# 44 of 80 edge tiles by one-hot products and 36 by gathers, in a two-layer graph kernel on one Trainium2 core

## The chip, the cores and the metric

The kernel runs on one core of a Trainium2 chip. Its engines are TensorE (PE in the profile; PEld are its weight loads), VectorE (DVE), ScalarE (ACT), GpSimd (POOL) and SyncE (SP); SP and POOL issue the DMAs here, and POOL alone the indirect ones (gathers and scatters by a list of row numbers). The metric is the device time of one execution in microseconds, lower is better: the median over the runs shown.

## What is computed

The reference is a two-layer graph transformer for 625 nodes, 512 features and 10,000 edges: layer 0 is a GENConv network, a linear attention and a small mixture of experts, layer 1 a graph attention, a second linear attention and a second mixture of experts, each with layer norms and residual sums. The change touches the scores of the graph attention of layer 1 (8 heads of 64):

```python
hr_src = h_r[:, src]
hr_dst = h_r[:, dst]
diff = hr_dst - hr_src
score = s_src + s_dst + jnp.einsum('hed,hd->he', diff, a_dif) \
    + jnp.einsum('hed,hd->he', jnp.abs(diff), a_abs) \
    + jnp.einsum('hed,hd->he', hr_src * hr_dst, a_prd)
alpha = jax.nn.leaky_relu(score, negative_slope=ALPHA)
m = jax.ops.segment_max(alpha.T, src, num_segments=N)
...
out = jax.ops.segment_sum(msg, src, num_segments=N)
```

The terms in `s_src`, `s_dst`, `a_dif` and `a_prd` are made for all pairs of nodes by dense products. The term with `abs(diff)` is not separable; it is made edge by edge, 125 edges a tile, 80 tiles. A score tile is [125 edges, 8 heads].

## The kernel before, in words

All engines run hand-written instruction streams that wait on semaphores. Five node tiles of 125 rows (`NT`), four column tiles of 128 (`KC`) and eight heads (`H`) make up the dense parts. The stage of the change is the loop over the edges in layer 1, `TURNS = ET // 2 = 40` turns, and each turn makes two tiles, one in each of two ways:

- **By gathers (chain 0).** POOL's `gather(g)` (L654) issues two indirect DMAs (L657) that fetch the rows of `h_r` for the sources (`gs`) and the destinations (`gd`) of 125 edges from the DRAM tensor `table`, four tiles ahead (`GATHERS`). DVE subtracts them (L1822), takes `max(.,0)` times the weights (`weighted_rise`, L1798) and sums each head into a slot of `sc` (`score`, L1806).
- **By one-hot products (chain 1).** DVE makes two one-hot matrices of the edges (L1789, L1792), PE turns their difference (`edge_turn`, L919), ACT copies it to SBUF (L1248), PE multiplies it with `h_r` in two halves, high and low (`edge_product`, L932), and DVE does `weighted_rise` and `score` on the result in PSUM.

POOL then scatters each score tile (`scatter`, L667) to one of two DRAM tables, `pairs_0` from the gathered tiles and `pairs_1` from the products; each table has one row for each pair of nodes. A scatter waits for its score and for the landing of the previous scatter into the same table (`scattered_0`, `scattered_1`), so the scatters of each table form a chain. POOL's order in a turn is: the scatter of chain 0, the two gathers for four turns later, the scatter of chain 1.

Beside the edges PE does the second linear attention: the tables of turns at L91 to L98 say in which turn it makes the keys, queries, values, the context, the heads' outputs, the turned rows for the next stage (`rT`) and the output projection (`PROJECTED`, five tiles `y1`, of which the last two stand behind the last turn). DVE adds each projected tile to `x` (`mix1_out`, L1780 and L1782). These tiles share two PSUM slots in turn, so a tile waits until the one two places before it has been emptied.

When both chains have landed, SP loads the tables back (L532 on), and DVE merges the two with a maximum, head by head (`merge`, L1854), before the softmax over all pairs of nodes (L1869 on).

## Time and profile before

| | |
|---|---|
| median of 3 runs | 1159.93 us (1158.28, 1159.93, 1166.69) |
| the profiled execution | 1156.4 us, of which the span of the trace is 1154.5 |
| PE busy | 1003.5 us (87%), 4204 matmuls |
| DVE busy | 785.5 us (68%) |
| POOL busy | 358.2 us (31%) |
| ACT busy | 325.6 us (28%) |
| edge stage, first gather to last scatter | 698.2 to 920.4 us |
| first merge of the two tables | 934.37 us |
| chain of work that ended last, by engine | PE 47%, DVE 25%, POOL 11%, issue 8%, DMA 7% |

The time of the profiled execution is its span and 1.9 us around it. Times in rows are microseconds from the start of the span. A row of the timeline gives start, length, engine, line, operation, what it writes and reads, and in brackets the idle time of that engine before it with what ended it; rows that follow one another closely are merged ("x8"). The chain of work that ended last is followed back from the last instruction, each step to what released it. "issue" is time in which an engine waited for nothing that the profile shows.

### The profile page before, as it was taken

How to read it: one execution, taken by the hardware profiler on the slowest of the kernel's cores; microseconds unless marked ns; L12 is line 12 of the kernel's file. 1: busy time of each engine (PE TensorE's matmuls, PEld its weight loads, DVE VectorE, ACT ScalarE, POOL GpSimd, SP SyncE). 2: the span in 40 equal slices, each digit the busy share in tenths (PEclk: the TensorE clock that was granted, in tenths of full speed). 3: DMA queues.
4: the chain of work that ended last, by engine and by line, in shares of the span. 5: the costliest groups of instructions: out<-in, count | busy, mean ns of one | idle time of the engine just before them, and what ended most of it. 6: DMA issues, size and time to landing. Idle time of an engine off the chain costs nothing.

```text
span 1154.5 us, 11857 instructions
## 1 busy us (share of the span) xinstructions
PE 1003.5 (87%) x4204; PEld 662.7 (57%) x4204; DVE 785.5 (68%) x1315; ACT 325.6 (28%) x569; POOL 358.2 (31%) x321
## 2 busy tenths in 40 slices
PE   6779988999989998999896987999859748888888
PEld 6655487644475444744463435776547427777754
DVE  8994496534587566954435377998878659998742
ACT  5682264311400123022013111321114204333411
POOL 4471800000020102001000116777777614343300
PEclk9989995999999999999897897999989867888999
DMA  9997020021410024001120325333333295422001
GB/s 293 307 309 237 0 100 1 1 90 37 153 37 0 1 90 136 1 0 53 45 109 1 118 44 156 93 95 103 100 93 93 61 416 202 178 90 78 19 1 45
DMA packets 65314, 115.08 MB, mean 100 GB/s; under 512 B 11393, under 2 KB 43393, under 8 KB 63341
## 3 DMA queue, kind: packets, MB, share of 16 engines
q1 hardware_dynamic: 56301, 93.08, 23.8%
q0 software_dynamic: 8960, 21.31, 6.5%
q8 instruction: 32, 0.52, 0.2%
q14 instruction: 21, 0.17, 0.0%
HBM read 85.88 MB, written 28.49 MB: 99 GB/s over the span
## 4 chain that ended last, share of the span: by engine, by line
PE 47%; DVE 25%; POOL 11%; issue 8%; DMA 7%; ACT 1%; DVEq 0%; SPq 0%; POOLq 0%
PE ps L713 19%; PE ps L849 8%; POOL arena L657 6%; PE ps L722 5%; DMA pairs<-arena,pairi 5%; DVE arena L1530 4%; PE ps L705 4%; POOL pairs L667 4%; DVE arena L1869 3%; PE ps L747 2%; DMA arena<-pairs 2%; PE ps L899 2%; PE ps L1050 2%; PE ps L1025 2%; PE ps L785 2%
## 5 line engine op out<-in xcount | busy, mean ns | idle before, releaser
L713 PE MATMUL ps<-arena 128*125 128x512 f32 x400 | 179.1, 603 | 0.0
L586 POOL TENSOR_TENSOR small<-small 125x1 f32<-125x1 f32 x50 | 33.0, 661 | 441.5 <-DVE small L1344 441.5
L705 PE MATMUL ps<-ident,arena 125*128 125x125 f32 (+3 forms) x545 | 85.5, 299 | 54.2 <-DVE small L1869 17.3
L713 PE MATMUL ps<-arena,xnT 128*125 128x512 f32 x280 | 127.6, 614 | 4.2 <-DVE x L1782 4.2
L713 PEld LDWEIGHTS ps<-arena 128*125 128x125 f32 x400 | 75.2, 192 | 89.0 <-issue 89.0
L705 PEld LDWEIGHTS ps<-ident,arena 125*128 125x128 f32 (+3 forms) x545 | 73.8, 176 | 86.2 <-issue 41.4
L932 PE MATMUL ps<-ex_low,high 125*125 125x512 f32 x400 | 108.5, 419 | 0.0
L1208 ACT ACTIVATE arena<-ps,cols 128x125 f32<-128x125 f32 x120 | 43.2, 465 | 214.6 <-PE ps L705 214.6
L667 POOL DMA_INDIRECT pairs<-arena,pairi x80 | 88.7, 1109 | 25.5 <-issue 25.5
L713 PEld LDWEIGHTS ps<-arena,xnT 128*125 128x125 f32 x280 | 54.1, 195 | 70.8 <-issue 70.3
L688 POOL TENSOR_TENSOR arena<-arena,counts 125x625 f32<-125x625 f32 x40 | 57.9, 1448 | 104.1 <-ACT arena L1313 104.1
L722 PE MATMUL ps<-arena 66*125 66x313 f32 (+3 forms) x176 | 63.3, 489 | 25.6 <-DVE small L1869 16.8
L932 PEld LDWEIGHTS ps<-ex_low,high 125*125 125x125 f32 x400 | 75.0, 195 | 16.9 <-issue 0.5
L747 PE MATMUL ps<-arena 125*125 125x314 f16 x400 | 62.8, 318 | 20.6 <-DVE arena L1387 19.6
L1062 ACT ACTIVATE arena<-ps 125x625 f32<-125x625 f32 (+4 forms) x79 | 49.3, 647 | 110.5 <-PE ps L705 102.6
L849 PE MATMUL ps<-arena 128*125 128x512 f32 x160 | 70.5, 593 | 1.7 <-DVE arena L1535 1.7
L747 PEld LDWEIGHTS ps<-arena 125*125 125x125 f16 x400 | 56.6, 147 | 26.6 <-DVE arena L1387 23.4
L1313 ACT ACTIVATE arena<-arena,small 125x625 f32<-125x625 f32 x40 | 32.7, 817 | 108.6 <-DVE arena L1878 108.6
L1591 DVE TENSOR_TENSOR x<-x,ps 125x512 f32<-125x512 f32 x30 | 20.5, 685 | 59.7 <-PE ps L713 23.4
L1025 PE MATMUL ps<-arena 125*125 125x96 f32 x400 | 57.7, 300 | 0.0
L1806 DVE TENSOR_REDUCE arena<-arena 125x8 f32<-125x512 f32 x80 | 54.6, 682 | 3.1 <-DMA pairs<-arena,pairi 1.7
L722 PEld LDWEIGHTS ps<-arena 66*125 66x125 f32 (+1 forms) x176 | 34.7, 217 | 37.3 <-DVE small L1869 18.5
(214 smaller groups left out, 1771.5 us busy)
## 6 DMA issues: line engine op xcount, KB each, us to landing
pairs<-fill SPq DMA_DIRECT2D x10, 2500.0 KB, 22.1
arena<-pairs SPq DMA_DIRECT2D x5, 2500.0 KB, 11.2
arena<-pairs SPq DMA_DIRECT2D x10, 1250.0 KB, 6.2
arena<-in_mw SPq DMA_DIRECT2D x6, 2048.0 KB, 8.4
arena<-in_rows SPq DMA_DIRECT2D x16, 250.0 KB
arena<-in_qkv_w SPq DMA_DIRECT2D x1, 3072.0 KB
arena<-in_cw SPq DMA_DIRECT2D x3, 1024.0 KB, 5.5
arena<-in_w_qkvT SPq DMA_DIRECT2D x1, 3072.0 KB
```

What stands on the lines that cost most here:

```text
L657: pool.indirect_dma_start(out=rows[:, g % GATHERS, :], out_offset=None, in_=table, in_offset=bass.IndirectOffsetOnAxis(ap=ends[:, 2 * g:2 ...
L667: pool.indirect_dma_start(out=pairs[n], out_offset=bass.IndirectOffsetOnAxis(ap=pairi[:, t:t + 1], axis=0), in_=sc[:, t % SCORES, :], in_o ...
L688: pool.tensor_tensor(Sg, Sg, counts[:, i, 0:N].bitcast(F32), ALU.mult).then_inc(sig("pair_weighted"), 1)
L705: last = pe.transpose(slot[0:n, at:at + rows], src, ident[0:rows, 0:rows])
L713: last = mm(slot[0:m, lo:hi], lhsT_of(k), rhs_of(k)[:, lo:hi], start=(k == 0), stop=(k == ks - 1))
L722: last = mm(slot[0:m, at + lo:at + hi], lhsT_of(k), rhs_of(k)[:, lo:hi], start=(k == 0), stop=(k == ks - 1))
L747: last = mm(ps[0:P, 512 * i:512 * i + HALF], one_hot[:, k, 0, P * i:P * (i + 1)], one_hot[:, k, 1, 0:HALF], start=False, stop=False, skip_ ...
L849: last = mm(slot[0:P, lo:lo + 512], nodes(hT, i)(k), w1[:, k, lo:lo + 512], start=(k == 0), stop=(k == KC - 1))
L932: last = mm(product_at[0:P, at:at + D], hotsT[e % 2][:, i, :], part[:, i, :], start=(part is hr_high and i == 0), stop=(part is hr_low and ...
L1025: last = mm(sums[0:P, at:at + WIDE], exTh[:, (i * H + h) % TURNED, P * k:P * (k + 1)], hea[:, v0:v0 + WIDE], start=(k == 0), stop=(k == NT ...
L1062: return act.activation(dst, src, ACT.Copy)
L1806: v.tensor_reduce(sc[0:P, t % SCORES, :], src.rearrange("p (h e) -> p h e", h=H), AX_X, ALU.add)\
```

## The change

The one-hot way makes 44 tiles and the gathers 36. There are 44 turns; a turn has a gathered tile beside it where `gathered_beside(e)` gives one, and none in the eight turns 0, 5, 11, 16, 22, 27, 33 and 38. The edges' columns are divided anew: tiles 0 to 43 are chain 1 and tiles 44 to 79 chain 0, where they alternated before. Each chain has four of the eight slots of `sc`, as before. The tables of turns move: the values, the keys' turns, the context and all behind it come one or two turns later, and of the five projection tiles three, not two, stand behind the last turn. In lines of the changed kernel a gather is L667 and a scatter L678, `edge_turn` L932, `edge_product` L945, a projection L726.

```diff
-TURNS = ET // 2
+TURNS = 44
+GATHERED = ET - TURNS
...
-VALUES = (16, 18, 19, 21, 23)
-KEYS_TURNED = (24, 25, 26, 27)
-CONTEXT = 29
-ATTENDED = (30, 31, 32, 33)
-ROWS_TURNED = (32, 33, 34, 35, 36, 37, 38, 39)
-PROJECTED = (34, 36, 38, TURNS, TURNS + 1)
+VALUES = (17, 19, 21, 23, 25)
+KEYS_TURNED = (26, 27, 28, 29)
+CONTEXT = 31
+ATTENDED = (32, 33, 34, 35)
+ROWS_TURNED = (34, 35, 36, 37, 38, 39, 40, 41)
+PROJECTED = (38, 41, TURNS, TURNS + 1, TURNS + 2)
+
+
+def gathered_beside(e):
+
+    q = e * GATHERED // TURNS
+    return q if (e + 1) * GATHERED // TURNS > q else None
...
-            for n in range(2):
-                sp.wait_ge(sig(f"scattered_{n}"), 16 * TURNS)
+            sp.wait_ge(sig("scattered_0"), 16 * GATHERED)
+            sp.wait_ge(sig("scattered_1"), 16 * TURNS)
...
-            def scatter(g, n):
-                t = 2 * g + n
-                pool.wait_ge(sig("product_scored" if n else "gather_scored"), g + 1)
-                if g:
-                    pool.wait_ge(sig(f"scattered_{n}"), 16 * g)
+            def scatter(n, k):
+
+                pool.wait_ge(sig("product_scored" if n else "gather_scored"), k + 1)
+                if k:
+                    pool.wait_ge(sig(f"scattered_{n}"), 16 * k)
+                t = k if n else TURNS + k
...
-            for g in range(GATHERS):
-                gather(g)
-            for g in range(TURNS):
-                scatter(g, 0)
-                if g + GATHERS < TURNS:
-                    gather(g + GATHERS)
-                scatter(g, 1)
+            for q in range(GATHERS):
+                gather(q)
+            for e in range(TURNS):
+                q = gathered_beside(e)
+                if q is not None:
+                    scatter(0, q)
+                    if q + GATHERS < GATHERED:
+                        gather(q + GATHERS)
+                scatter(1, e)
...
-            pe.wait_ge(sig("gather_scored"), TURNS)
+            pe.wait_ge(sig("gather_scored"), GATHERED)
...
-                t = slice(2 * e + 1, 2 * e + 2)
+                t = slice(e, e + 1)
...
-                v.wait_ge(sig(f"gathered_{k}"), 32 * (g // GATHERS + 1))
-                TT(gd[0:P, k, :], gd[0:P, k, :], gs[0:P, k, :], ALU.subtract)\
-                    .then_inc(sig("differences"), 1)
+                if q is not None:
+                    gq, gq_src = gd[0:P, q % GATHERS, :], gs[0:P, q % GATHERS, :]
+                    v.wait_ge(sig(f"gathered_{q % GATHERS}"), 32 * (q // GATHERS + 1))
+                    TT(gq, gq, gq_src, ALU.subtract).then_inc(sig("differences"), 1)
                 v.wait_ge(sig("product_weighted"), g + 1)
-                score(dif, g, 1)
-                v.wait_ge(sig("differences"), g + 1)
-                weighted_rise(gd[0:P, k, :], gd[0:P, k, :], "gather_weighted")
-                v.wait_ge(sig("gather_weighted"), g + 1)
-                score(gd[0:P, k, :], g, 0)
+                score(dif, 1, g)
+                if q is not None:
+                    v.wait_ge(sig("differences"), q + 1)
+                    weighted_rise(gq, gq, "gather_weighted")
+                    v.wait_ge(sig("gather_weighted"), q + 1)
+                    score(gq, 0, q)
```

The order of POOL's indirect DMAs around the turns 3 to 5, before; in brackets the semaphores that an instruction waits for (`scattered_1` is the landing of the scatter before it in chain 1):

```order
L667 DMA pairs<-arena,pairi 400000x8 [waits scattered_0,gather_scored]
L657 DMA arena<-table,srci 128x512
L657 DMA arena<-table,dsti 128x512
L667 DMA pairs<-arena,pairi 400000x8 [waits scattered_1,product_scored]
L667 DMA pairs<-arena,pairi 400000x8 [waits scattered_0,gather_scored]
L657 DMA arena<-table,srci 128x512
L657 DMA arena<-table,dsti 128x512
L667 DMA pairs<-arena,pairi 400000x8 [waits scattered_1,product_scored]
```

The same engine around the turns 4 to 6 of the changed kernel:

```order
L678 DMA pairs<-arena,pairi 400000x8 [waits scattered_0,gather_scored]
L667 DMA arena<-table,srci 128x512
L667 DMA arena<-table,dsti 128x512
L678 DMA pairs<-arena,pairi 400000x8 [waits scattered_1,product_scored] x2
L678 DMA pairs<-arena,pairi 400000x8 [waits scattered_0,gather_scored]
L667 DMA arena<-table,srci 128x512
L667 DMA arena<-table,dsti 128x512
L678 DMA pairs<-arena,pairi 400000x8 [waits scattered_1,product_scored]
```

Before, scatters of chain 1 always had a scatter of chain 0 and two gathers between them; now two of them stand in direct succession ("x2") in seven places. At the very end both kernels have nine scatters and no gather left.

PE at the end of the edges, before: the last two products (L932), turned rows (L705) and projection tiles (L713; `vector_emptied` and `scalar_emptied` are PSUM slots that DVE or ACT must have emptied), then the first product of the next stage (L722):

```order
L713 MATMUL ps<-arena,xnT 125x512 [waits scalar_emptied,wo1_loaded]
L713 MATMUL ps<-arena,xnT 125x512 x3
L932 MATMUL ps<-ex_low,high 125x512 [waits product_weighted,hotsT_ready]
L932 MATMUL ps<-ex_low,high 125x512 x9
L705 MATMUL ps<-ident,arena 66x125 [waits scalar_emptied]
L705 MATMUL ps<-ident,arena 66x125 x4
L713 MATMUL ps<-arena,xnT 125x512 [waits vector_emptied,wo1_loaded,scalar_emptied]
L713 MATMUL ps<-arena,xnT 125x512 x3
L713 MATMUL ps<-arena,xnT 125x512 [waits scalar_emptied,wo1_loaded]
L713 MATMUL ps<-arena,xnT 125x512 x3
L722 MATMUL ps<-arena 125x312 [waits scalar_emptied,vector_emptied,product_scored,gather_scored]
```

The same place of the changed kernel (products L945, projection tiles L726, next stage L735):

```order
L945 MATMUL ps<-ex_low,high 125x512 [waits product_weighted,hotsT_ready]
L945 MATMUL ps<-ex_low,high 125x512 x9
L726 MATMUL ps<-arena,xnT 125x512 [waits scalar_emptied,wo1_loaded]
L726 MATMUL ps<-arena,xnT 125x512 x3
L726 MATMUL ps<-arena,xnT 125x512 [waits vector_emptied,wo1_loaded,scalar_emptied]
L726 MATMUL ps<-arena,xnT 125x512 x3
L726 MATMUL ps<-arena,xnT 125x512 [waits vector_emptied,wo1_loaded,scalar_emptied]
L726 MATMUL ps<-arena,xnT 125x512 x3
L735 MATMUL ps<-arena 125x312 [waits scalar_emptied,vector_emptied,product_scored,gather_scored]
```

Three projection tiles, not two, now stand between the last edge product and the next stage, and the first of them waits for ACT alone.

## Rows read from the trace of the kernel before

**Rows 1.** Stretches: PE, PEld, DVE, ACT, POOL busy (xinstructions), granted clock, DMA share, GB/s

```profile
706.00:784.00 78.00, 76.48 (x364) 57.87 (x363) 71.82 (x116) 21.17 (x33) 60.93 (x57) 1.00 0.36 102
706.00:913.00 207.00, 186.12 (x878) 134.90 (x877) 178.35 (x292) 52.24 (x77) 161.49 (x149) 0.97 0.35 98
```

**Rows 2.** Scatters and source gathers: duration ns min/median/max, first and last start; scatters' landing

```profile
L667 POOL DMA_INDIRECT pairs<-arena,pairi x80: 971/1002/1632, 709.2 to 920.4; - x80
...
DMA to landing us min/median/max: 2.1/2.4/4.9
...
L657 POOL DMA_INDIRECT arena<-table,srci x40: 946/987/1586, 698.2 to 905.9; - x40
```

**Rows 3.** Timeline of POOL over one turn in the middle of the stage

```profile
796.57 1.00 POOL L667 DMA_INDIRECT pairs<-arena,pairi  x1 [0.30 <-issue]
797.88 1.00 POOL L667 DMA_INDIRECT pairs<-arena,pairi  x1 [0.30 <-issue]
799.18 1.27 POOL L657 DMA_INDIRECT arena<-table,srci  x1 [0.30 <-DMA pairs<-arena,pairi]
800.76 0.96 POOL L657 DMA_INDIRECT arena<-table,dsti  x1 [0.30 <-issue]
```

**Rows 4.** Timeline of POOL at the end: scatters of chain 1 among the last

```profile
914.74 0.97 POOL L667 DMA_INDIRECT pairs<-arena,pairi  x1 [0.57 <-issue]
...
917.58 0.97 POOL L667 DMA_INDIRECT pairs<-arena,pairi  x1 [0.56 <-issue]
...
920.42 0.97 POOL L667 DMA_INDIRECT pairs<-arena,pairi  x1 [0.56 <-issue]
```

**Rows 5.** Chain of waits: start, length (of a DMA to its landing), what

```profile
796.57 2.46 DMA pairs<-arena,pairi
...
920.42 2.11 DMA pairs<-arena,pairi
...
923.02 11.26 DMA arena<-pairs
```

**Rows 6.** Timeline: scores of turns 0 and 6, turn 0's scatter, turn 6's start on DVE

```profile
708.06 0.69 DVE L1806 TENSOR_REDUCE arena<-arena 125x8 f32<-125x512 f32 x1
...
709.20 1.63 POOL L667 DMA_INDIRECT pairs<-arena,pairi  x1 [0.30 <-issue]
...
735.60 0.69 DVE L1798 SCALAR_TENSOR_TENSOR arena<-ps,arena 125x512 f32<-125x512 f32 x1 [1.27 <-PE ps L932]
...
738.11 0.69 DVE L1806 TENSOR_REDUCE arena<-arena 125x8 f32<-125x512 f32 x1
```

**Rows 7.** Timeline: a one-hot instruction of DVE and a scatter that starts in it

```profile
713.55 0.87 DVE L1792 SCALAR_TENSOR_TENSOR arena<-arena 125x625 f16<-125x625 f16 x1
713.68 1.62 POOL L667 DMA_INDIRECT pairs<-arena,pairi  x1 [0.30 <-issue]
```

**Rows 8.** Timeline: projection tiles on PE, DVE's last addition and first merges

```profile
895.79 3.60 PE L713 MATMUL ps<-arena,xnT 128*125 128x512 f32 x8
...
917.99 10.05 PE L713 MATMUL ps<-arena,xnT 128*125 128x512 f32 x16 [4.24 <-DVE x L1782]
...
928.87 0.69 DVE L1782 TENSOR_TENSOR x<-x,ps 125x512 f32<-125x512 f32 x1
934.37 5.91 DVE L1854 TENSOR_TENSOR arena<-arena 125x625 f32<-125x625 f32 x8 [4.82 <-DMA arena<-pairs]
```

**Rows 9.** PE: a bare turn, the last product, and its longest waits (total, times, longest)

```profile
802.18 0.45 PE L919 MATMUL ps<-arena 125*125 125x125 f16 x5
...
804.85 0.45 PE L919 MATMUL ps<-arena 125*125 125x125 f16 x5
...
910.33 2.88 PE L932 MATMUL ps<-ex_low,high 125*125 125x512 f32 x10
...
PE ps L722 <- DVE arena L1772: 8.8, 1, 8.8
PE ps L919 <- DVE arena L1792: 4.9, 4, 1.9
```

More of the change, by code:

```diff
@@ L652, in _, with gather @@
             pool.wait_ge(sig("pairs_filled"), 16 * 2 * (NP // 128))
[L654 removed]
+            def gather(q):
+                t = slice(TURNS + q, TURNS + q + 1)
                 for rows, ends in ((gs, srci), (gd, dsti)):
                     pool.indirect_dma_start(
[L658 to L666 removed]
+                        out=rows[:, q % GATHERS, :], out_offset=None, in_=table,
+                        in_offset=bass.IndirectOffsetOnAxis(ap=ends[:, t], axis=0)
+                    ).then_inc(sig(f"gathered_{q % GATHERS}"), 16)
+            def scatter(n, k):
[3 more added lines that the diff above has]
+                t = k if n else TURNS + k
                 pool.indirect_dma_start(
@@ L1812, in _ @@
             for g in range(TURNS):
-                k, dif = g % GATHERS, difs[g % 2]
+                dif, q = difs[g % 2], gathered_beside(g)
                 if g + 2 < TURNS:
```

16 lines of the change are left out of this document (6 added, 10 removed).

## The prediction

> **What bounds the kernel now.** I read the engine totals first: PE is busy 87% of the span and everything else less, which says nothing about this change, because the change touches one stage only, the 40 turns of edges from 698 to 922 us. So the next view is the stretches of that stage. In the first part of it, 706 to 784 us, PE is busy 76.5 of 78 us; over the whole of 706 to 913 us it is busy 186.1 of 207, so 20.9 us are idle [rows 1]. PE is dense, then, yet it does not set the end. POOL's instructions do. It issues 160 indirect DMAs, 40 gathers by source, 40 by destination and 80 scatters, the first at 698.2 and the last at 920.4 [rows 2]: 222.2 us for 159 steps, 1.398 us a step. POOL's timeline of one turn shows no wait: scatter, scatter, gather, gather, each about 1.0 us with 0.30 us between, so the next turn's scatter can begin at 800.76 + 0.96 + 0.30 = 802.02 and the turn has taken 5.45 us [rows 3]. The reader should see that those 0.30 us are "issue" and not a wait for a score (the one that names a landing is no longer than the others): VectorE (DVE) is ahead. The chain of waits then runs from POOL's last scatter over its landing to a load of 11.26 us [rows 5], and DVE's first merge at 934.37 waits for that load [rows 8]. So whatever moves POOL's last scatter (920.42) moves the end of the kernel by as much, unless something else is later than 934.37.
>
> **Removed.** Four gathered tiles fewer are eight gathers fewer. The scatters stay 80 (44 and 36). 152 steps instead of 160 at 1.398 us: -11.2 us.
>
> **Added: waits inside a chain.** A scatter waits until the one before it in its own chain has landed. Now the two chains alternate, and a chain's next scatter comes a whole turn later, when that landing is long past. After the change eight turns have no gathered tile: 0, 5, 11, 16, 22, 27, 33 and 38. Turn 0 costs nothing, since nothing is ahead of it. In the seven others POOL's queue holds two scatters of chain 1 in direct succession, as the order shows. The price has to come from two rows. The last turns of the kernel before already have nothing but scatters in the queue, and there chain 1 starts one every 2.84 us (914.74, 917.58, 920.42) [rows 4]; such a scatter lands 2.11 us after its start [rows 5], so 2.84 - 2.11 = 0.73 us pass from landing to the next start. In the middle of the stage, behind two gathers, the landing takes 2.46 us [rows 5]. So the second scatter starts 2.46 + 0.73 = 3.19 us after the first; without the wait it would be 1.00 + 0.30 = 1.30 [rows 3]. A wait of 1.89 us, seven times: +13.2 us. The bounds are the landings: 2.1 us at least gives 1.53 us a wait, 4.9 at most gives 4.33 [rows 2]. I take 1.89, near the median landing of 2.4.
>
> The Trainium skill, "DMA: Bandwidth & Descriptors", section "Anatomy of one DMA — SWDGE (gpsimd) path", speaks against the change in the same way: a DMA issued from GpSimd has a fixed cost of about 2.0 us, nearly all of it the wait for the receipt of the write. By its 2.0 us the wait would be an estimated 2.0 + 0.73 - 1.30 = 1.43 us and the seven 10.0 us; the trace has the longer landing, and the sum goes by the trace.
>
> **Added: POOL catches up with DVE at the start.** The first gathered tile is now scored in turn 1, not in turn 0, and POOL has less to do in the first turns, while DVE's scores come no sooner, because PE makes them at its own pace there [rows 1]. In the kernel before the score of turn 0 ended at 708.75 and its scatter began at 709.20, 0.45 us later [rows 6]. The score of turn 6's gathered tile ended at 738.80 [rows 6], so after the change its scatter cannot start before 739.25. How early would POOL be there? Ahead of it stand 8 gathers, turn 0's scatter, four turns of four and turn 5's scatter, 26 steps: 698.2 + 26 x 1.398 + 1.89 = 736.4. So POOL has to wait 2.8 us in these turns: +2.8 us. From 739.25 on, 126 DMAs are left, 125 steps of 1.398 = 174.8, and six of the seven chain waits, 11.3: the last scatter starts at **925.3 us**, 4.9 us later than now. The three terms say the same: -11.2 + 13.2 + 2.8 = +4.8.
>
> **PE and DVE.** A turn without extra work costs PE 2.67 us (802.18 to 804.85) [rows 9]. Four more are 10.7 us; one projection tile, 3.60 us [rows 8], moves out behind the edges; so PE's last edge product, which ends at 913.21 [rows 9], would end at 913.2 + 7.1 = 920.3 if its 20.9 idle us stay as they are. I cost this at nothing: POOL's last turn starts about 922.5 by the sum above. It is a thin cover, about 2 us, and if PE is later than that, each us goes into the end. On DVE a gathered tile taken away is three instructions and a one-hot tile added is four, of about 0.7 us each [rows 6], so four tiles add some 3 us to an engine that is idle 28.6 of the 207 us [rows 1] and that POOL trails: nothing.
>
> **The third projection tile behind the edges.** Two such tiles take 10.05 us now, 5.0 each, and the last addition of DVE ends at 929.56, 4.8 us before the merges [rows 8]. With three, PE ends at 920.3 + 15.1 = 935.4 and DVE about 1.5 us later (929.56 against 928.04 now), 937; the merges start 934.37 - 920.42 = 13.95 us after the last scatter, at 939.3. So it is covered by 2.3 us; uncovered it costs what sticks out. The order shows that the first two tiles no longer wait for DVE, which they did for 4.24 us [rows 8]. The other edits (columns, slots of the scores, the counts that SP waits for) keep their work; SP waits for both chains as before, and the later one, chain 1, decides.
>
> **The sum.** +4.9 us on the profiled execution's own time of 1156.4 us (its span of 1154.5 and 1.9 around it): 1161.3. The median of the runs shown, 1159.93, is 3.5 us above that execution, so I forecast **1165 us** for a median: 0.4% more, no change that can be told.
>
> **Rivals.** *A, the chain waits cost little* (POOL has other time to lose there, or landings are past). POOL alone would then end at 739.25 + 174.8 = 914.0, 6.4 us early. But the last scores are not there: if PE loses the 4.9 us in which it now waits for one-hots [rows 9], its last product ends at 915.4; DVE's part of a turn takes 3.2 us (735.60 to 738.80) [rows 6], 0.45 us later the first of the last two scatters starts and 1.3 us after it the other, at 920.4. So 1154 to 1160 us. For it: gathers could fill the gap; against it: the rows of the tail, where the wait is paid each time, and the order, in which nothing stands between the two scatters. *B, long landings,* the one that ends slower: a landing behind gathers can take 4.9 us [rows 2]; seven waits of 4.33 instead of 1.89 are +17 us, 1182 us. It passes the 1% from a mean landing of about 3.4 us on. Against it: the median of 2.4. *C, VectorE's one-hots block more descriptors.* The scatter at 713.68 takes 1.62 us instead of 1.00, when a one-hot instruction of DVE starts at 713.55 [rows 7]. Such stretches are in my 1.398 us (1.00 + 0.30 would be 1.30, so 0.10 a step). Should each of the 44 one-hot pairs hit one DMA in full, 44 x 0.62 = 27.3 us against 152 x 0.10 = 15.2: +12 us, 1177. Against it: now 40 pairs cost 16 us, a good half of that. *D, PE or the third tile is late* and eats its cover: another 2 to 5 us, 1167 to 1170; for it: 8.8 us in which PE waits for the context [rows 9], which do not go away.
>
> The Trainium skill, "SBUF — State Buffer", section "Who interferes with whom", has the rule behind C: a DVE instruction in a two-port mode and GpSimd exclude each other, so descriptors are not written while it runs. [...]
>
> **How the numbers follow.** The forecast 0.65, with a range of its own of 1160 to 1170 (a chain wait from 1.53 to 2.3, a step from 1.37 to 1.42 us); A 0.15, B 0.07, C 0.05, D 0.08. The range 1156 to 1172 holds the forecast, D and most of A and leaves out B and C. One per cent, 11.6 us, is about what a measurement of this kernel tells from no change: slower by more is B, C and a tail of D, 0.11; faster by more than that needs POOL's end 11.6 us early, which PE's products forbid, 0.02; within it, 0.87.
>
> **What would show it.** In POOL's timeline seven gaps of about 2.2 us between two scatters (0.30 + 1.89), behind the turns 5, 11, 16 and so on; waits of 3 us together before turn 7; a mean step that is otherwise still about 1.39 us; the last scatter at 925 us in the span; merges 14 us later, waiting for the load and not for DVE's additions. Gaps of 0.30 would make A right, gaps above 3 us B, a larger mean of the DMAs themselves C, and a merge that waits for the projection D.

## The result, and the profile after

The changed kernel takes **1167.86 us** (median of 17 executions, 1159.99 to 1177.92); the kernel before, timed beside it, 1160.72 us. The ratio is 1.0062 with a 95% interval of 1.0037 to 1.0087: 4 to 10 us slower, 7 in the middle. The ratio and all means below leave out executions more than 1.5% above the fastest of their kernel, here one of 1177.92 us after and one of 2034.77 us before. The forecast was 1165 us, the range 1156 to 1172, and "within 1%" held; but the 7 us are not the 4.9 us of the prediction's sum, and finding out what they are was the work of the runs below.

| | before | after |
|---|---|---|
| profiled execution | 1156.4 us | 1169.94 us (span 1168.1) |
| first gather to start of last scatter | 222.2 us | 224.3 us |
| first merge, counted from the last scatter | 13.95 us | 14.50 us |
| first merge to end of the last head's rise on DVE | 151.7 us | 162.3 us |
| from there to the end | 68.4 us | 70.1 us |
| PE, POOL busy | 1003.5, 358.2 us | 1025.9, 345.3 us |

The third line from the bottom is the surprise. It is the pair stage, the softmax over all pairs of nodes; a "rise" is the product of one head in it, which PE makes and DVE takes in. Its code is the same in both kernels, and it grew by 10.6 us; the edge stage, to which the whole change belongs, grew by 2.1.

First the edge stage. Scatters and source gathers in the changed kernel (duration ns min/median/max, first and last start), to be read against [rows 2]:

```profile
L678 POOL DMA_INDIRECT pairs<-arena,pairi x80: 968/999/1627, 707.6 to 921.2; - x80
...
DMA to landing us min/median/max: 2.1/2.4/4.2
```

```profile
L667 POOL DMA_INDIRECT arena<-table,srci x36: 945/992/1589, 696.9 to 905.8; - x36
```

POOL's timeline, those of its scatters that had waited (in brackets, with the usual 0.30 in it): the start of the stage, then the second scatter of each pair in direct succession.

```profile
709.68 0.98 POOL L678 DMA_INDIRECT pairs<-arena,pairi  x1 [1.05 <-DVE arena L1819]
716.65 0.99 POOL L678 DMA_INDIRECT pairs<-arena,pairi  x1 [2.12 <-DVE arena L1819]
734.66 1.40 POOL L678 DMA_INDIRECT pairs<-arena,pairi  x1 [2.15 <-DMA pairs<-arena,pairi]
737.39 0.97 POOL L678 DMA_INDIRECT pairs<-arena,pairi  x1 [1.33 <-DMA pairs<-arena,pairi]
766.30 0.99 POOL L678 DMA_INDIRECT pairs<-arena,pairi  x1 [2.20 <-DMA pairs<-arena,pairi]
791.24 0.99 POOL L678 DMA_INDIRECT pairs<-arena,pairi  x1 [2.25 <-DMA pairs<-arena,pairi]
821.48 0.99 POOL L678 DMA_INDIRECT pairs<-arena,pairi  x1 [1.99 <-DMA pairs<-arena,pairi]
846.51 0.99 POOL L678 DMA_INDIRECT pairs<-arena,pairi  x1 [2.33 <-DMA pairs<-arena,pairi]
877.75 0.99 POOL L678 DMA_INDIRECT pairs<-arena,pairi  x1 [2.26 <-DMA pairs<-arena,pairi]
903.12 0.99 POOL L678 DMA_INDIRECT pairs<-arena,pairi  x1 [1.90 <-DMA pairs<-arena,pairi]
...
918.10 1.25 POOL L678 DMA_INDIRECT pairs<-arena,pairi  x1 [0.59 <-DVE arena L1819]
```

All seven gaps stand where the order had put them, at turns 5, 11, 16, 22, 27, 33 and 38: the rows from 734.66 to 903.12 without the one at 737.39. Without the 0.30 us they wait 1.60 to 2.03 us, 13.0 us together. In two of the rows the releaser that is named had nothing to do with it. The scatter at 737.39, of turn 6's gathered tile, starts 0.28 us after its own score. The last row's scatter, at 918.10, had its own score 4.6 us earlier and starts 0.75 us after the landing of the scatter before it in its chain, as its neighbours in the tail do. So POOL's chain of landings sets the last scatter here. But DVE is right behind it: the score of the last gathered tile ends at 919.23 and its scatter starts at 919.65, 0.42 us later, where the shortest such distance in this stage is 0.28.

```profile
736.43 0.69 DVE L1819 TENSOR_REDUCE arena<-arena 125x8 f32<-125x512 f32 x1
...
918.54 0.69 DVE L1819 TENSOR_REDUCE arena<-arena 125x8 f32<-125x512 f32 x1
...
919.65 1.02 POOL L678 DMA_INDIRECT pairs<-arena,pairi  x1 [0.30 <-issue]
```

In the kernel before the same distance is 2.36 us, so there the second limit lies 2.1 us behind POOL:

```profile
915.84 0.69 DVE L1806 TENSOR_REDUCE arena<-arena 125x8 f32<-125x512 f32 x1
...
918.89 0.97 POOL L667 DMA_INDIRECT pairs<-arena,pairi  x1 [0.34 <-issue]
```

The chain of waits across the end of the stage (start, length, what), to be read against [rows 5], shows what DVE waited for in turn:

```profile
905.37 3.44 PE ps L726 x8
908.80 0.29 PE ps L932 x5
909.09 2.40 PE ps L945 x10
...
916.03 0.68 DVE arena L1811
...
921.22 2.71 DMA pairs<-arena,pairi
...
924.43 11.20 DMA arena<-pairs
```

A projection tile (L726, 3.44 us) stands on PE ahead of the last products, then come DVE's scores, the last scatter, its landing and the load. (The chain passes to DVE by the releaser named at 918.10; over the landings it would run along POOL and end in the same scatter.)

Then the pair stage. Stretches of PE (length, busy, matmuls, granted clock, DMA share, GB/s). Before, from 23 us behind the first merge to the end of the last rise, and a piece of it:

```profile
957.40:1086.10 128.70, 111.82 (x656) 0.86 0.33 122
```

```profile
958.00:961.00 3.00, 3.00 (x15) 0.50 0.84 327
962.00:976.00 14.00, 13.88 (x96) 1.00 0.44 163
```

After, the same stretch, and its two long pieces at the lower level:

```profile
958.70:1098.00 139.30, 123.33 (x656) 0.79 0.30 112
```

```profile
960.00:977.00 17.00, 17.00 (x66) 0.50 0.32 114
...
1037.00:1060.00 23.00, 23.00 (x88) 0.50 0.16 56
```

The same 656 matmuls take 123.3 us of PE instead of 111.8, because for 17 and for 23 us on end TensorE runs at 0.50, the lower of its two levels (1.2 GHz instead of 2.4), although it is busy all of that time. What DVE waits for in the stretch (total us, times, longest), before and after:

```profile
DVE arena L1869 <- PE ps L722: 5.3, 5, 1.3
```

```profile
DVE arena L1884 <- PE ps L735: 16.0, 11, 2.3
```

DVE is busy 120.9 us of the stretch before and 120.8 after, so the 10.7 us more that it waits for rises are the whole growth of the stage in these two profiles, 10.6 us. So the question for the runs was twofold: what sets the end of the edge stage now, and does the change have anything to do with the clock 40 to 140 us behind it?

### The profile page after: what moved, and what is told of

Read it like the earlier page. It is cut to its first block, busy times and chain, and to the rows that moved or that the text cites. A ratio compares the mean times of both kernels' runs of the same rounds, so it can differ in the third digit from the quotient of the medians.

```text
span 1168.1 us, 11993 instructions
## 1 busy us (share of the span) xinstructions
PE 1025.9 (88%) x4264; PEld 681.6 (58%) x4264; DVE 786.0 (67%) x1319; ACT 328.8 (28%) x573; POOL 345.3 (30%) x313
## 4 chain that ended last, share of the span: by engine, by line
PE 49%; DVE 26%; POOL 8%; issue 8%; DMA 7%; ACT 1%; DVEq 0%; SPq 0%; POOLq 0%
PE ps L726 20%; PE ps L862 8%; PE ps L735 6%; DMA pairs<-arena,pairi 5%; POOL arena L667 4%; PE ps L718 4%; DVE arena L1543 4%; DVE arena L1884 3%; POOL pairs L678 2%; PE ps L1038 2%; PE ps L760 2%; DMA arena<-pairs 2%; PE ps L912 2%; PE ps L1063 2%; DVE arena L1893 2%
## 5 line engine op out<-in xcount | busy, mean ns | idle before, releaser
L726 PE MATMUL ps<-arena 128*125 128x512 f32 x400 | 180.1, 606 | 0.0
L718 PE MATMUL ps<-ident,arena 125*128 125x125 f32 (+3 forms) x545 | 88.3, 306 | 50.0 <-DVE small L1884 16.5
L726 PEld LDWEIGHTS ps<-arena 128*125 128x125 f32 x400 | 75.5, 193 | 89.6 <-issue 89.6
L718 PEld LDWEIGHTS ps<-ident,arena 125*128 125x128 f32 (+3 forms) x545 | 76.7, 182 | 83.4 <-issue 40.8
L726 PE MATMUL ps<-arena,xnT 128*125 128x512 f32 x280 | 123.0, 596 | 0.0
L945 PE MATMUL ps<-ex_low,high 125*125 125x512 f32 x440 | 116.5, 412 | 0.0
L678 POOL DMA_INDIRECT pairs<-arena,pairi x80 | 85.3, 1067 | 43.0 <-issue 21.4
L735 PE MATMUL ps<-arena 66*125 66x313 f32 (+3 forms) x176 | 69.9, 531 | 28.5 <-DVE small L1884 22.1
L945 PEld LDWEIGHTS ps<-ex_low,high 125*125 125x125 f32 x440 | 81.2, 193 | 17.8
L726 PEld LDWEIGHTS ps<-arena,xnT 128*125 128x125 f32 x280 | 52.6, 189 | 64.2 <-issue 63.7
L1075 ACT ACTIVATE arena<-ps 125x625 f32<-125x625 f32 (+4 forms) x79 | 49.4, 649 | 125.7 <-PE ps L718 119.4
L1884 DVE CUSTOM_DVE_ANT_0 arena<-ps,arena 125x625 f32<-125x625 f32 x40 | 51.4, 1285 | 16.1 <-PE ps L735 16.0
L735 PEld LDWEIGHTS ps<-arena 66*125 66x125 f32 (+1 forms) x176 | 37.7, 235 | 41.6 <-DVE small L1884 23.8
L1038 PE MATMUL ps<-arena 125*125 125x96 f32 x400 | 61.8, 314 | 0.0
```

The costliest lines, as they stand in the source:

```text
L678: pool.indirect_dma_start(out=pairs[n], out_offset=bass.IndirectOffsetOnAxis(ap=pairi[:, t:t + 1], axis=0), in_=sc[:, n * SCORES // 2 + k ...
L718: last = pe.transpose(slot[0:n, at:at + rows], src, ident[0:rows, 0:rows])
L726: last = mm(slot[0:m, lo:hi], lhsT_of(k), rhs_of(k)[:, lo:hi], start=(k == 0), stop=(k == ks - 1))
L735: last = mm(slot[0:m, at + lo:at + hi], lhsT_of(k), rhs_of(k)[:, lo:hi], start=(k == 0), stop=(k == ks - 1))
L945: last = mm(product_at[0:P, at:at + D], hotsT[e % 2][:, i, :], part[:, i, :], start=(part is hr_high and i == 0), stop=(part is hr_low and ...
L1038: last = mm(sums[0:P, at:at + WIDE], exTh[:, (i * H + h) % TURNED, P * k:P * (k + 1)], hea[:, v0:v0 + WIDE], start=(k == 0), stop=(k == NT ...
```

## The experiments

In the table, "stage" is first gather to start of last scatter; "last product" the start of PE's last matmul of an edge product, counted from the first gather; "pair" first merge to end of the last rise; "at 0.50" the time at the lower clock in it, from 23 us behind the first merge, summed over slices of 2 us as 2 x (1 - granted clock) x 2 us, good to about 1 us. All of these are of the one profiled execution of each run. The "median" is that of the timed ones, 17 of before and after and 12 of each other run that is not marked (one). The runs behind "after" were timed in three sessions (again, spread, two_behind, warm; light, light_spread, filled, filled_before; the other four), each with the kernel before beside them, so across sessions the ratios compare better than the medians.

| run | stage | last product | pair | at 0.50 | median | ratio to before |
|---|---|---|---|---|---|---|
| before | 222.2 | 214.6 | 151.7 | 35.6 | 1160.72 | |
| before_again | 220.5 | 212.9 | 151.7 | 35.5 | 1153.05 (one) | |
| after | 224.3 | 216.5 | 162.3 | 56.4 | 1167.86 | 1.0062 (1.0037 to 1.0087) |
| again | 224.8 | 216.5 | 161.1 | 65.4 | 1168.40 | 1.0086 (1.0046 to 1.0126) |
| again_third | 226.6 | 216.8 | 159.4 | 57.0 | 1168.95 (one) | |
| spread | 224.1 | 216.5 | 154.3 | 38.2 | 1161.96 | 1.0028 (0.9992 to 1.0063) |
| two_behind | 225.4 | 218.0 | 153.2 | 43.9 | 1166.17 | 1.0048 (1.0017 to 1.0079) |
| warm | 225.6 | 217.7 | 155.3 | 49.4 | 1164.14 | 1.0025 (0.9989 to 1.0061) |
| light | 225.5 | 210.5 | 151.4 | 31.7 | 1160.67 (one) | |
| light_spread | 213.4 | 202.8 | 155.4 | 42.7 | 1150.32 (one) | |
| filled | 224.3 | 216.5 | 147.6 | 0.0 | 1154.47 | 0.9962 (0.9933 to 0.9992) |
| filled_spread | 224.0 | 216.4 | 147.7 | 0.0 | 1156.61 | 0.9985 (0.9955 to 1.0016) |
| filled_before | 220.5 | 212.9 | 147.4 | 0.0 | 1150.23 | 0.9931 (0.9903 to 0.9959) |
| filled_before_third | 220.3 | 210.0 | 149.9 | 12.4 | 1153.14 | 0.9945 (0.9907 to 0.9982) |

### What sets the end of the edge stage

**spread.** The seven waits are taken off POOL by its order alone:

```diff
             for e in range(TURNS):
                 q = gathered_beside(e)
+                next_bare = e + 1 < TURNS and gathered_beside(e + 1) is None
                 if q is not None:
                     scatter(0, q)
+                    if next_bare:
+                        scatter(1, e)
                     if q + GATHERS < GATHERED:
                         gather(q + GATHERS)
-                scatter(1, e)
+                if q is None or not next_bare:
+                    scatter(1, e)
```

> The changed kernel, with the chain-1 scatter of the turn before a turn without a gathered tile put ahead of that turn's two gathers, so that no two scatters of chain 1 stand in direct succession on POOL (but for nothing else). Takes away seven waits of 1.85 us (13.0 us) on POOL. Theory 'POOL and TensorE meet at the end': the last product of TensorE ends at 913.8 and VectorE's last score at 919.2 in any case, and the last scatter starts 2 us behind it, so the stage gets no shorter than about 222.5 us and the whole 0 to 2 us faster than the changed kernel (ratio to before 1.002 to 1.007), with POOL idle in the last turns for VectorE's scores. Rival 'POOL bounds the stage to its end': 13 us come off the edge stage, 211 us, ratio to before 0.993 to 0.997.

The stage took 224.1 us, so 13 us less waiting on POOL bought 0.2 us. POOL's last scatters in this kernel:

```profile
916.96 1.16 POOL L678 DMA_INDIRECT pairs<-arena,pairi  x1 [3.68 <-DVE arena L1823]
918.43 0.97 POOL L678 DMA_INDIRECT pairs<-arena,pairi  x1 [0.30 <-issue]
921.40 1.16 POOL L678 DMA_INDIRECT pairs<-arena,pairi  x1 [2.00 <-DVE arena L1823]
```

And what POOL waited for in the stage altogether (total us, times, longest):

```profile
POOL pairs L678 <- DVE arena L1823: 17.2, 10, 3.7
```

The waits have not gone, they have changed their name: POOL is now ahead and waits 17.2 us (0.30 of each in it) for DVE's scores, which wait for PE's products. The scatter at 921.40 starts 0.28 us after its score, so here DVE sets the end. The last product starts 216.5 us after the first gather with the chain waits and without them. The median came out 6 us lower than the changed kernel's, which the stage does not explain; the pair stage was shorter in the profile (154.3 us), and more on that stands below.

**light** and **light_spread.** The other side: PE is relieved instead of POOL, in the changed kernel and in spread.

```diff
-                for part in (hr_high, hr_low):
-                    for i in range(NT):
-                        last = mm(product_at[0:P, at:at + D], hotsT[e % 2][:, i, :],
-                                  part[:, i, :], start=(part is hr_high and i == 0),
-                                  stop=(part is hr_low and i == NT - 1))
+                for i in range(NT):
+                    last = mm(product_at[0:P, at:at + D], hotsT[e % 2][:, i, :],
+                              hr_high[:, i, :], start=(i == 0), stop=(i == NT - 1))
```

> The changed kernel with only the five products of the high part in a turn (the five of the low part are left out of every turn, so TensorE has some 1.3 us a turn less). Theory 'POOL and TensorE meet at the end': VectorE's scores come long before POOL wants them, POOL alone sets the stage, first gather to start of last scatter 220 to 223 us, 1 to 4 us less than with all products. Rival 'TensorE bounds the changed edge stage': 205 to 215 us.

> The same with the chain-1 scatters spread as in the run before on it, so that the seven waits on POOL are gone too. Theory 'POOL and TensorE meet at the end': now neither holds the stage, 207 to 213 us (seven waits of 1.85 us less than with the light products alone). Rival 'the waits cost nothing, POOL has something else to wait for': 217 to 223 us as with the light products alone.

The scatters' rows of both:

```profile
L678 POOL DMA_INDIRECT pairs<-arena,pairi x80: 966/999/1629, 709.9 to 924.8; - x80
```

```profile
L678 POOL DMA_INDIRECT pairs<-arena,pairi x80: 967/999/1623, 707.8 to 910.6; - x80
```

With half the products the stage took 225.5 us, no less than with all of them. The expected 220 to 223 was too low. POOL's waits at the start did go away, as I had counted on: its 27th DMA starts 38.6 us after the first, not 40.5. But two of the seven gaps came out at 2.88 and 3.19 us, and the steps behind them took 1.40 instead of 1.38 us. With half the products and no chain waits the stage took 213.4, just above the expected 207 to 213. So this is a case of two limits that meet: POOL alone needs 225 us, PE and DVE alone 224 us. Relieving one gives nothing, relieving both gives 12.1 us, which is also the cost of the seven waits when nothing hides it: 1.73 us each. (Each of these two is one execution.)

**filled_spread** repeats the first test where the clock of the pair stage cannot disturb it (its edit is that of "filled", below, and that of spread together).

> The changed kernel with the added products of the run 'filled' and with the chain-1 scatters spread as in the run 'spread': with the pair stage at the full clock throughout, executions differ little, and a gain of 2 us would show. Theory 'POOL and TensorE meet at the end': the seven waits are gone from POOL, TensorE's last product stands where it stood, the edge stage stays at 224 us and the whole at 1153 to 1156 us (1154.5 with the waits). Rival 'the waits cost what POOL loses by them': 13 us less, 1141 to 1144 us.

1156.61 us against 1154.47 us with the waits, which was timed in another session; the ratios to the kernel before, 0.9985 and 0.9962, overlap in their intervals. The stage took 224.0 against 224.3 us. The 13 us are not in the time.

**two_behind.** The third projection tile goes back among the edges:

```diff
-PROJECTED = (38, 41, TURNS, TURNS + 1, TURNS + 2)
+PROJECTED = (36, 38, 40, TURNS, TURNS + 1)
```

> The changed kernel, with the third projection tile back among the edges (at turns 36, 38 and 40; two behind). Theory 'the third tile is covered but the products are nearly the end': TensorE's last product moves 3.6 us later (917 us), VectorE's last score to 922 or 923, the last scatter to 924 or 925: 2 to 4 us slower than the changed kernel (ratio to before 1.007 to 1.012). Rival 'POOL bounds the stage to its end': the same time as the changed kernel in the edge stage. Rival 'the third tile behind the edges is late': 1 to 4 us faster, since the first rise of the pair stage and its clock start earlier.

The last product starts 1.5 us later (218.0), the stage is 1.1 us longer than in the changed kernel's first profile (225.4), inside the 224.3 to 226.6 us of its three. The expected sign is there and half the size, and the last gathered tile's scatter starts 0.27 us after its score, so DVE sets the end here. The median is 1.7 us below the changed kernel's, again with the shorter pair stage. Whether three tiles behind the edges are better than two with 44 turns is not settled by the medians; the clock of the timed executions, below, speaks for three.

**filled_before_third.** One part of the change alone, in the kernel before with the added products of "filled":

```diff
-PROJECTED = (34, 36, 38, TURNS, TURNS + 1)
+PROJECTED = (34, 37, TURNS, TURNS + 1, TURNS + 2)
```

> The kernel before with the added products and with three projection tiles behind the edges instead of two (at turns 34 and 37, then 40 to 42): one part of the change alone. Theory 'the third tile is covered': TensorE has 3.6 us less ahead of its last product, the last add of the tile ends some 1 to 3 us ahead of the first merge, and POOL sets the edge stage as before or 1 to 2 us earlier: 1148 to 1151 us (1150.2 with two). Rival 'the third tile is late': the first merge or the first rise waits for it, 1152 to 1155 us.

The tile is covered: DVE's last addition for it starts 11.4 us ahead of the first merge, which waits for the load.

```profile
921.90 0.69 DVE L1793 TENSOR_TENSOR x<-x,ps 125x512 f32<-125x512 f32 x1
933.32 5.91 DVE L1865 TENSOR_TENSOR arena<-arena 125x625 f32<-125x625 f32 x8 [10.74 <-DMA arena<-pairs]
```

PE's last product came 2.9 us earlier (210.0) and the stage stayed at 220.3 us: in the kernel before, POOL alone set it. The whole still came out 2.9 us slower than filled_before, though in another session and with ratios that overlap (0.9945 and 0.9931). The profile shows 1.0 us more in the load (12.33 instead of 11.35 us) and 2.5 us more in the pair stage, where the added products, laid out for another start, let the clock fall once more (12.4 us at 0.50). The time lies above the 1148 to 1151 us of the theory, in the range of the rival, but not by the rival's way. So as a test of time this run is inconclusive; as a test of the cover it is clear.

### What the clock of the pair stage has to do with it

**again**, **again_third**, **before_again.** Both kernels once more, unchanged.

> The changed kernel itself, a second time. In its profiled execution the edge stage grew by 2.1 us (first gather to start of last scatter, 222.2 to 224.3 us), while the stretch from the first merge to the end grew by 12.3 us (220.1 to 232.4 us) though no line of it was changed: TensorE's granted clock stood at 0.50 from 959.5 to 978 us and from 1034 to 1060 us, where before it stood so from 956 to 961 and from 1028 to 1032. Theory 'own course': which bursts of the pair stage run at the half clock differs from execution to execution; this run's stretch behind the first merge then lies somewhere else between 220 and 233 us, and the edge stage again within 1 us of 224.3. Rival 'fixed course': the changed start of the stage sets it; then the two long stretches at 0.50 come back at the same places and the rest is again 230 to 234 us. The ratio to before is 1.004 to 1.009 by both.

> The changed kernel itself, a third time, for the same. Theory 'own course': anywhere from 30 to 65 us at 0.50 in the pair stage, 150 to 163 us long. Rival 'the change sets it': 55 to 65 us again, 160 to 163 us.

> The kernel before itself, a second time, for the clock of its pair stage. Theory 'own course': the time at 0.50 in the pair stage differs from execution to execution (35.6 us and 151.7 us of pair stage in the first); here it lies anywhere from 30 to 65 us, and the stage at 139 us plus 0.37 of it, 150 to 163 us. Rival 'the change sets it': 30 to 45 us again, 150 to 156 us, while both executions of the changed kernel had 56 and 65.

The stretch from 23 us behind the first merge to the end of the last rise, PE, in again, again_third and before_again, beside 0.86 and 0.79 in the rows above:

```profile
958.60:1096.70 138.10, 126.23 (x656) 0.76 0.31 113
```

```profile
960.60:1097.00 136.40, 122.53 (x655) 0.79 0.30 114
```

```profile
954.00:1082.70 128.70, 111.69 (x656) 0.86 0.33 122
```

"Own course" holds for the places: in again the long piece at 0.50 lies at 985 to 1005 us, in the changed kernel's first profile at 1037 to 1060. The sum looks fixed in these profiles: 56, 65 and 57 us in three executions of the changed kernel, 35.6 and 35.5 in two of the kernel before, and 159 to 162 against 151.7 us of pair stage. But five profiles are few, and the timed executions say otherwise. Each of them has its granted clock on record, as a mean over the span:

| | executions | granted clock, lowest to highest | mean | at 0.50 over the whole span |
|---|---|---|---|---|
| before, its two profiles | 2 | 0.923, 0.925 | | 177, 173 us |
| before, timed beside the runs | 75 | 0.908 to 0.925 | 0.917 | 192 us |
| after and again | 28 | 0.906 to 0.927 | 0.916 | 197 us (193 and 201) |
| spread | 12 | 0.911 to 0.925 | 0.920 | 185 us |
| two_behind | 12 | 0.912 to 0.925 | 0.919 | 189 us |

(The last column is 2 x (1 - granted clock) x span.) So the sum does jump from execution to execution, in both kernels over nearly the same range, and the two profiles of the kernel before lie at the upper end of its own. The times go with it: fitted over the 103 executions of the two kernels, each us more at 0.50 comes with 0.36 us more time. The mean difference of the two kernels, 5 us at 0.50, is then worth some 2 us. But in the profiles the edge stage of the changed kernel has 9 us less at 0.50 (16 us instead of 24 and 26), where PE does not set the end; the rest of its span then has some 14 us more, worth 5 us. Both are estimates from these numbers. I read it as: the changed kernel loses 2 to 5 us more to the clock, and the 10.6 us of the first two profiles overstate it.

The same numbers bear on two runs above. Spread has 16 us less at 0.50 than again, timed beside it: an estimate of 5.6 us of the 5.9 us between their means, so nothing is left for the 13 us of waits. Two_behind has 12 us less, worth 4.3, and is only 2.5 us faster in the mean; at the same clock it would be some 2 us slower than the changed kernel, as expected.

**warm.** The first attempt to take the clock out of it: TensorE gets products of the identity with itself to do at the start of the pair stage.

```diff
+            def keep_busy(n):
+                for _ in range(n):
+                    mm(sums[0:128, 0:128], ident[:, :], ident[:, :], start=True, stop=True,
+                       skip_group_check=True)
+
+            keep_busy(32)
             for g in range(NT * H + LAG + TURNED_LAG):
                 i, h = divmod(g, H)
+                if g in (3, 4):
+                    keep_busy({3: 10, 4: 4}[g])
...
+                if g == LAG:
+                    keep_busy(8)
                 i, h = divmod(g - LAG, H)
```

> The changed kernel, with TensorE given products of the identity with itself to do where it idles at the start of the pair stage (32 ahead of the first rise, 10, 4 and 8 between the first rises), into the bank of the head sums, which the first head's sums overwrite. Nothing else reads them. Theory 'the clock makes the pair stage long': the first bursts of the pair stage (5 transposes, 10 sums, 4 rises) then run at the granted clock 1.00 instead of 0.50, 2.7 us a head instead of 5.2, and the stretch from first merge to end comes to 217 to 224 us; 4 to 10 us faster than the changed kernel, ratio to before 0.997 to 1.003. Rival 'the pair stage goes by VectorE and the loads': no change from the changed kernel, 1.004 to 1.009. Rival 'the added products come late': they still run when the rises are wanted, some us slower.

1164.14 us, 4 us under the changed kernel, inside what was expected; but not by the way that was expected. There was still a wait of 5.58 us on PE that the few added products did not fill, and the clock was at 0.50 behind it:

```profile
945.19 2.45 PE L735 MATMUL ps<-arena 66*125 66x312 f32 x4 [5.58 <-DVE small L1895]
```

(Four matmuls of a rise in 2.45 us; at the full clock they take 1.25.) With 49.4 us at 0.50 the run shows nothing about what the clock costs.

**filled** and **filled_before.** PE's waits for DVE in the pair stage, here those of the kernel before (total us, times, longest), are filled all through the stage, in the changed kernel and in the kernel before.

```profile
PE ps L705 <- DVE small L1869: 16.2, 9, 3.4
```

```diff
+            def keep_busy(n, b=0):
+                for _ in range(n):
+                    mm(sums[0:128, 512 * b + HW:512 * (b + 1)], ident[:, :], ident[:, :],
+                       start=True, stop=True, skip_group_check=True)
+
+            keep_busy(32)
             for g in range(NT * H + LAG + TURNED_LAG):
                 i, h = divmod(g, H)
+                keep_busy({3: 32, 4: 18}.get(g, 0))
...
+                keep_busy({4: 14, 5: 3}.get(g, 0))
+                if 10 < g < NT * H:
+                    keep_busy({7: 11, 3: 3}.get(g % H, 0), int(g % H == 3))
                 i, h = divmod(g - LAG, H)
```

> The changed kernel, with products of the identity with itself (0.23 us each at the full clock, nothing reads them) where TensorE waits in the pair stage for VectorE: 32 ahead of the first rise, 32, 18, 14 and 3 between the first ones, and in each later round of eight heads 11 ahead of one turn and 3 ahead of another, where the trace shows waits of 3.4 and 1.0 us for VectorE. Theory 'idle, then half clock': the waits are what the granted clock falls after, so the clock stays at 1.00 in most of the pair stage, the time at 0.50 in it falls from 56 to 65 us (both executions of the changed kernel) to under 25, and with 0.37 us of pair stage for each us of it (151.7 us at 35.6, 162.3 at 56.4) the stretch from the first merge to the last rise comes to 140 to 150 us: 1148 to 1158 us in all, ratio to before 0.989 to 0.997. Rival 'the clock falls by its own': time at 0.50 as before, 155 to 163 us, and the added products make it 0 to 10 us longer.

> The kernel before with the same added products in the same places. Theory 'idle, then half clock': 1143 to 1155 us, ratio 0.985 to 0.995, and between this and the changed kernel with them only the edge stage's 2 to 3 us are left (0.997 to 0.998). Rival 'the change costs 7 us somewhere else than in the edge stage and the pair stage's clock': the two still differ by 6 to 8 us.

The same stretch of the pair stage in filled and in filled_before:

```profile
957.80:1082.40 124.60, 113.42 (x781) 1.00 0.34 126
```

```profile
953.80:1078.20 124.40, 112.92 (x776) 1.00 0.34 126
```

The clock stays at 1.00 from end to end; 125 and 120 matmul rows more, for products that nobody needs, make the pair stage 4 us shorter than that of the kernel before and 15 us shorter than that of the changed one, and equal in both, 147.6 and 147.4 us. (The 0.37 us of stage for each us at 0.50, by which I had expected 140 us and more, does not reach down to zero: in filled DVE is busy 122.0 of the 124.6 us and waits for nothing. Nor do the two points quoted for it give 0.37; they give 0.51.) What is left between the two kernels is then in the main the edge stage: 1154.47 - 1150.23 = **4.2 us**, with an uncertainty of some 2 us, and the profiles say the same, 224.3 - 220.5 = 3.8 us of stage and 0.5 us more from the last scatter to the first merge. That is more than the 2 to 3 us expected and less than the 6 to 8 of the rival. And both are faster than the two kernels of the case; the kernel before with the added products is the fastest that was run, 0.9931 (0.9903 to 0.9959).

The Trainium skill, "TensorE: Matmul & The Clock Gate", section "HAM oscillation — how this bites in real kernels", tells of a matmul kernel whose TensorE waits for a DMA after each block, is put back to the lower clock in every one of these waits, and starts every block at the lower clock. This pair stage agrees, with VectorE in the place of the DMA: pauses filled, 0.0 us at 0.50; pauses left, 32 to 65 us. What the rows here show beyond it is the return: 17 and 23 us of PE busy without a break, at 0.50 throughout.

## Why the prediction was right, and where it was not

**Eight gathers fewer and the steps.** Right in kind. From the scatter of turn 6's gathered tile (737.39) to the last scatter (921.22) pass 183.83 us; without six chain waits (11.1 us) 172.7, over 125 steps 1.382 us. The prediction took 1.398 from [rows 2], and that is the mis-sized term: 125 x 0.016 = 2.0 us too much. Fewer DMAs were stretched: 17 of the 152 took more than 1.3 us, where before it was 26 of 160. About two thirds of the 2.0 us belong to the one execution that the step was read from: before_again has 21 stretched DMAs and a step of 1.387.

**The seven chain waits.** Right: +13.2 us forecast, 13.0 measured in the gaps, 12.1 when they were taken away in the kernel with half the products. The way to the price, the landing of one scatter plus the distance from landing to the next start in the tail, carried over from [rows 4, 5] to places where no such wait had ever been.

**POOL catches up at the start.** Right: that scatter was to come no earlier than 739.25, 41.1 us after the first gather; it came 40.5 us after it (696.91), and in again and again_third as well. It started 0.28 us after its score (the row at 736.43), where the sum took 0.45, and the three waits for scores up to there, without the 0.30 us, come to 3.6 us; the sum had 2.8.

**The edge stage.** +4.9 us forecast. Measured +2.1 us between the two profiles first compared, +3.9 us between the means of three and two (225.2 and 221.35), +4.2 us in the time with the clock held. That a median of 1167.86 us lies in the forecast's own range of 1160 to 1170 is in part luck: by subtraction 3 of its 7 us come from a place that the sum does not have.

**PE costs nothing, under a thin cover.** Right that it adds nothing to the sum; the reading was off. PE's last product was put at up to 920.3; it ended at 913.80 (the row at 908.90, below), 216.9 us after the first gather and 1.9 us later than before, because PE took the added turns out of its idle time, 16.4 us in 706 to 914 us instead of 20.9 [rows 1]:

```profile
706.00:784.00 78.00, 76.13 (x366) 57.76 (x365) 65.69 (x107) 21.23 (x33) 54.65 (x53) 1.00 0.33 91
706.00:914.00 208.00, 191.63 (x927) 140.52 (x926) 176.09 (x290) 55.88 (x82) 147.57 (x141) 0.98 0.31 86
```

But behind that product DVE still had the additions of a projection tile and two pairs of scores ahead of the last scatter, and so PE and DVE set an end at 224 us, where POOL set one at 225. The cover that I put at 2 us was 0.1 us in this profile (0.42 - 0.28) and 2.2 us at most in the three; spread shows that there were two limits, as far apart as one execution is from the next.

**Rival A, "the waits cost little".** Wrong in its ground (no gap was 0.30 us) and in its time (1154 to 1160 us), right in the thing that matters to whoever wants to use it: taking away the whole 13 us of waits gains nothing, because of the last scores. Its price had PE end 217.2 us after the first gather and the last scatter start 5.0 us later. In spread PE ends at 216.9, as priced, but the last scatter starts 7.2 us later, since DVE has two pairs of scores and the additions of a projection tile to do in between. **B** and **C** did not occur: landings from 2.1 to 4.2 us, steps shorter and not longer. What C rests on is there: before, 21 of the 29 DMAs that start within the two-tensor one-hot instruction (L1792, 0.87 us) take more than 1.3 us, after 13 of 29. Of those that start within the one-tensor one (L1789, 0.38 us), 8 before and 11 after, none does. No row shows whether L1792 runs in a two-port mode, so the rule named behind C is not borne out here.

**The third tile.** Covered, by much more than the 2.3 us of the sum: [rows 8] had two tiles at 5.0 us each, part of them at the lower clock. In the changed kernel PE goes from the last product straight into the three tiles at the full clock, 3.57 us each, and DVE's addition is 10 us ahead of the merge:

```profile
908.90 4.90 PE L945 MATMUL ps<-ex_low,high 125*125 125x512 f32 x20
913.64 10.72 PE L726 MATMUL ps<-arena,xnT 128*125 128x512 f32 x24
```

```profile
925.20 0.69 DVE L1795 TENSOR_TENSOR x<-x,ps 125x512 f32<-125x512 f32 x1
935.72 5.90 DVE L1869 TENSOR_TENSOR arena<-arena 125x625 f32<-125x625 f32 x8 [9.84 <-DMA arena<-pairs]
```

**"Whatever moves POOL's last scatter moves the end by as much."** This is the step that failed. The last scatter moved by 0.8 us in the span and the end by 13.6 us. The prediction took everything behind the first merge as fixed, and looked at the clock of the edge stage only, where it is 0.97 to 1.00. The pair stage was already losing time to the lower clock before the change, and that loss is not the same from kernel to kernel. Of the 7.1 us between the medians, 4.2 are the edge stage by the pair of filled runs. The other 3 are by subtraction the clock's, a difference of two differences that are each uncertain by 2 to 3 us; that they are the clock's is supported by the profiles and by the 2 to 5 us estimated from the timed executions' clocks, and not shown. Why the changed kernel's pair stage should spend more time at 0.50, when spread and two_behind, whose pair stages begin in the same way, had 38 and 44 us in their one profile, stays open.

Not tried: moving the projection tile of turn 41 out from between the last products together with spread, which by the chain of waits might relieve both limits at once.

## What to carry to other kernels

Before an edit is priced on the engine that sets the end of a stage, ask how far behind it the next limit lies: here POOL at 225 us hid PE and DVE at 224, and only relieving both moved anything. A wait that a change adds can be priced well from rows that show its two parts elsewhere in the trace. And where TensorE pauses again and again for another engine, look at the granted clock of that stage before anything else: filling the pauses with products that nobody reads gave more than either arrangement of the edges. One profile of such a kernel is one draw: before a difference between two profiles is explained, compare the granted clocks of the timed executions.

## What the runs showed of the hardware

- TensorE stayed at 0.50 for 17 us (960 to 977 us) and for 23 us (1037 to 1060 us) in which it was busy all the time; elsewhere it came back after some 3 us (958 to 961 us in the kernel before).
- Pauses of 3.4 us and less on PE were enough to bring the lower clock back round after round. In the stretches of before, after, again and spread each of the 17 falls follows a pause of 1.6 to 3.4 us, while one pause of 2.2 us (1067 us in the changed kernel) was followed by none; with 11 and 3 products of 0.23 us in them, and 1.2 us as the longest pause left, it stayed at 1.00 for 124 us.
- An indirect scatter that must wait for the landing of the one before it started 3.0 to 3.5 us after its start in the seven places of the changed kernel, always 0.77 us behind the landing; in a tail that holds nothing but scatters it is 2.84 us, 0.73 behind the landing.
